# Attention with three PSUM banks for scores, three for the products behind the exponentials, and exponentials of 512 columns

## The reference, cut to what matters

```python
def _rmsnorm_global(x, scale):
    rms = jnp.sqrt(jnp.mean(x * x))
    return x / (rms + EPS) * scale
q, k, v = jnp.split(x @ Wqkv, 3, axis=-1)      # each reshaped to b, s, 16 heads, 16
q = _rmsnorm_global(q, scale_q)
k = _rmsnorm_global(k, scale_k)
attn = jnp.einsum('bqhd,bkhd->bhqk', q, k)
attn = jax.nn.softmax(attn, axis=-1)
z = jnp.einsum('bhqk,bkhd->bqhd', attn, v)
return z.reshape(b, s, d) @ Wo
```

## Time and profile before

| | |
|---|---|
| median of 3 runs | 1784.2 us (1782.71 to 1784.86) |
| profiled execution, its time | 1782.6 us |
| its span, first to last instruction | 1780.8 us |
| TensorE matmul busy | 1558.5 us, 88% of the span |
| VectorE busy | 859.6 us, 48% |
| ScalarE busy | 766.6 us, 43% |
| GpSimd busy | 488.2 us, 27% |
| mean granted TensorE clock | 0.931 |
| second attention | from 1010 to 1291 us of the span |

### The profile page before, as it was taken

The page is one execution under the profiler, slowest core; times in us unless marked ns, Lnnn a source line. Parts: engine busy times, 40 slices in busy tenths (PEclk is TensorE's granted clock), DMA queues, the critical chain, the costliest instruction groups (busy, mean ns, idle before and its releaser), DMA issues.

```text
span 1780.8 us, 19192 instructions
## 1 busy us (share of the span) xinstructions
PE 1558.5 (88%) x7128; PEld 881.8 (50%) x7128; DVE 859.6 (48%) x885; ACT 766.6 (43%) x1176; POOL 488.2 (27%) x139
## 2 busy tenths in 40 slices
PE   5887896698989987799887588888799999999998
PEld 3775333687979784554343222222254444444443
DVE  4994757698989886544430676666210000000000
ACT  1232565798989872113232146556622122122221
POOL 0996200398879790401022200000000000000000
PEclk7799898899999998589999689999989999999999
DMA  3000003122231115110100651111000000000000
GB/s 143 16 10 1 24 25 146 45 84 95 105 108 62 48 37 213 29 18 18 35 35 36 116 222 53 41 53 36 1 0 1 0 12 0 0 12 0 12 0 12
DMA packets 32078, 84.84 MB, mean 48 GB/s; under 512 B 5091, under 2 KB 21569, under 8 KB 29569
## 3 DMA queue, kind: packets, MB, share of 16 engines
q1 hardware_dynamic: 30081, 82.21, 13.5%
q10 hardware_dynamic: 1920, 1.57, 0.6%
HBM read 66.79 MB, written 16.91 MB: 47 GB/s over the span
## 4 chain that ended last, share of the span: by engine, by line
PE 55%; POOL 16%; DVE 9%; issue 8%; ACT 4%; DVEq 4%; DMA 1%; ACTq 1%; SPq 0%; POOLq 0%
POOL arena L2049 15%; PE ps L1223 13%; PE ps L1238 12%; PE ps L1095 3%; DVE mxs L1922 3%; PE ps L1007 3%; PE ps L1135 2%; PE ps L1075 2%; PE ps L1049 2%; DVE arena L1623 2%; PE ps L751 2%; DVEq L1622 2%; POOL arena L2029 2%; ACT arena L1548 1%; PE ps L964 1%
## 5 line engine op out<-in xcount | busy, mean ns | idle before, releaser
L2049 POOL TENSOR_TENSOR arena<-arena 128x2048 f32<-128x2048 f32 x64 | 289.9, 4559 | 166.6 <-DVE arena L1722 166.6
L1722 DVE TENSOR_TENSOR_SCAN arena<-arena,ps 128x1024 f32<-128x1024 f32 x128 | 283.9, 2270 | 45.7 <-issue 23.2
L1223 PE MATMUL ps<-arena 128*128 128x512 f32 x512 | 242.3, 599 | 0.0
L1238 PE MATMUL ps<-arena 128*128 128x512 f32 x512 | 239.3, 592 | 0.0
L1590 ACT ACTIVATE arena<-ps,arena 128x512 f32<-128x512 f32 x128 | 87.9, 687 | 349.4 <-PE ps L1223 349.3
L1922 DVE TENSOR_REDUCE mxs<-ps 128x1 f32<-128x512 f32 x256 | 162.0, 684 | 71.5 <-PE ps L1075 70.0
L1424 ACT ACTIVATE arena<-arena,mam 128x511 f32<-128x511 f32 x256 | 165.2, 708 | 33.3 <-DVE arena L1722 33.3
L1548 ACT ACTIVATE arena<-ps,rho 128x1024 f32<-128x1024 f32 x128 | 140.4, 1110 | 90.3 <-PE ps L1135 90.1
L2009 DVE SCALAR_TENSOR_TENSOR arena<-ps,b2s,arena 128x512 f32<-128x512 f32 x8 | 5.6, 747 | 334.4 <-PE ps L1238 334.4
L1223 PEld LDWEIGHTS ps<-arena 128*128 128x128 f32 x512 | 98.0, 192 | 121.9 <-issue 121.9
L1238 PEld LDWEIGHTS ps<-arena 128*128 128x128 f32 x512 | 97.3, 190 | 122.5 <-issue 122.5
(11 more groups left out here) (291 smaller groups left out, 1910.4 us busy)
## 6 DMA issues: line engine op xcount, KB each, us to landing
arena<-bc_scratch SPq DMA_DIRECT2D x32, 512.0 KB, 3.6
batch_scratch<-arena SPq DMA_DIRECT2D x2, 3072.0 KB, 9.1
arena<-batch_scratch SPq DMA_DIRECT2D x6, 1024.0 KB, 7.6
arena<-q_scratch SPq DMA_DIRECT2D x96, 64.0 KB, 2.1
arena<-in_cond SPq DMA_DIRECT2D x1, 5019.5 KB, 23.9
arena<-k_scratch SPq DMA_DIRECT2D x72, 64.0 KB, 2.1
mam<-in_ids SPq DMA_DIRECT2D x4, 768.0 KB, 7.3
q_scratch<-arena SPq DMA_DIRECT2D x4, 768.0 KB, 3.3
```

What stands on the lines that cost most here:

```text
L1223: last = pe.matmul(ps[:, 2 + f % 4, :], w1[:, c, f * P:(f + 1) * P], y4[:, b if isinstance(b, int) else bass.ds(b, 1), c, :], start=(c == ...
L1238: last = pe.matmul(ps[:, 6 * turn + o, :], w2[:, f - 2, o * P:(o + 1) * P], hid[:, (f - 2) % 4, :], start=(f == 2), stop=(f == FM + 1))
L1722: dve.tensor_tensor_scan(half, view(decay[:, (2 * k + h) % 3], [[1, 2 * S]]), view(ps[:, FEED + 2 * h, :], [[1, 2 * S]]), 0.0, ALU.mult, A ...
L2049: pool.tensor_tensor(state[:, k % SLOTS], state[:, k % SLOTS], view(c_rows[:, j % 2, k % G, :], [[0, M], [1, S]]), ALU.mult).then_inc(s_hc, 1)
```

## The change

The six banks are shared out anew: scores go to banks 0, 1 and 2 in turn, the products behind the exponentials to banks 3, 4 and 5 in turn. TensorE now alternates one product and one score, each product counts in `s_t_mm` by itself and waits for the exponential three before it, and each score for the maximum three before it. Exponentials are taken one bank at a time, 512 columns, and `s_pt` counts 16 in a group instead of 8. Sixteen isn't a multiple of three, so the turn is shifted by hg; at hg = 0 it starts anew, and the first product and the first score of that group wait for the one just before them. The counts that others wait for (SP's head loads, the matmul after the stage, `values`, `max_rows`) are adapted.

```diff
@@ SP: heads of the next batch
-                        sp.wait_ge(s_t_mm, g * 8 + 8)
+                        sp.wait_ge(s_t_mm, g * 16 + 16)
@@ TensorE: scores
-                pe.wait_ge(s_max, (b * HG + hg) * 16 + s + 1)
-                pe.matmul(ps[:, s % 2, :], qstack[0:STACK, hg, i, qc * P:(qc + 1) * P], kstack[0:STACK, hg, i, :],
+                if not isinstance(b, int) or b or hg or s > 2:
+                    pe.wait_ge(s_max, (b * HG + hg) * 16 + s + (1 if hg + s == 0 else -1))
+                pe.matmul(ps[:, (hg + s) % 3, :], qstack[0:STACK, hg, i, qc * P:(qc + 1) * P], kstack[0:STACK, hg, i, :],
                           start=True, stop=True).then_inc(s_s_mm, 1)
@@ TensorE: max_rows, values
-                pe.wait_ge(s_max, g * 16 + 18)
+                pe.wait_ge(s_max, g * 16 + 17)
...
-                pe.wait_ge(s_pt, g * 8 + 2 * kc + 4)
+                pe.wait_ge(s_pt, g * 16 + 4 * kc + 7)
@@ TensorE: attend
-                        pe.wait_ge(s_pt, g * 8 + j + 1)
                         for i in (2 * pair, 2 * pair + 1):
-                            last = pe.matmul(ps[:, 2 + 2 * pair + i % 2, :], kstack[0:STACK + 1, hg, i, kc * P:(kc + 1) * P],
-                                             qstack[0:STACK + 1, hg, i, :], start=True, stop=True)
-                        last.then_inc(s_t_mm, 1)
-                        if not (final and hg >= 2):
-                            scores(*ahead, 2 * j)
-                            scores(*ahead, 2 * j + 1)
+                            n = 4 * kc + i
+                            pe.wait_ge(s_pt, g * 16 + n + (3 if hg + n == 0 else 1))
+                            pe.matmul(ps[:, 3 + (hg + n) % 3, :], kstack[0:STACK + 1, hg, i, kc * P:(kc + 1) * P],
+                                      qstack[0:STACK + 1, hg, i, :], start=True, stop=True).then_inc(s_t_mm, 1)
+                            if not (final and hg >= 2):
+                                scores(*ahead, n)
@@ ScalarE: weigh (act.sem_inc(s_pt, 2) at the start becomes 3)
-                        n = g * 8 + j
-                        act.wait_ge(s_t_mm, n + 1)
-                        act.wait_ge(s_pv, g * TILES + j // 2)
-                        act.activation(pt[:, j % 4], ps[:, 2 + 2 * (j % 2):4 + 2 * (j % 2), :], ACT.Exp,
-                                       scale=rho[:, 0:1]).then_inc(s_pt, 1)
+                        for i in range(2):
+                            n = 2 * j + i
+                            act.wait_ge(s_t_mm, g * 16 + n + 1)
+                            act.wait_ge(s_pv, g * TILES + j // 2)
+                            act.activation(pt[:, j % 4, i], ps[:, 3 + (hg + n) % 3, :], ACT.Exp,
+                                           scale=rho[:, 0:1]).then_inc(s_pt, 1)
@@ VectorE: maximum (dve.sem_inc(s_max, 2) at the start becomes 1)
-                dve.tensor_reduce(mxs[:, hg % 2, qc, i:i + 1], ps[:, s % 2, :], AX, ALU.max).then_inc(s_max, 1)
+                dve.tensor_reduce(mxs[:, hg % 2, qc, i:i + 1], ps[:, (turn + s) % 3, :], AX, ALU.max).then_inc(s_max, 1)
```

More of the change, by code:

```diff
@@ L1186, in _ @@
             pe.wait_ge(s_ew, 16)
-            pe.wait_ge(s_pt, B * HG * 8 + 2)
+            pe.wait_ge(s_pt, B * HG * 16 + 3)
             for o in range(C):
@@ L1526, in _ @@
             act.activation(rho[:, :], rho[:, :], ACT.Exp, scale=0.5).then_inc(s_rho_root, 1)
-            act.sem_inc(s_pt, 2)
+            act.sem_inc(s_pt, 3)
             act.wait_ge(s_kp, B + 1)
@@ L1916, in _, with maximum @@
             dve.reciprocal(rho[:, 0:1], rho[:, 0:1]).then_inc(s_rho, 1)
-            dve.sem_inc(s_max, 2)
-            def maximum(hg, n, s):
+            dve.sem_inc(s_max, 1)
+            def maximum(hg, turn, n, s):
                 i, qc = s % HG, s // HG
                 dve.wait_ge(s_s_mm, n + s + 1)
-                dve.tensor_reduce(mxs[:, hg % 2, qc, i:i + 1], ps[:, s % 2, :], AX, ALU.max).then_inc(s_max, 1)
+                dve.tensor_reduce(mxs[:, hg % 2, qc, i:i + 1], ps[:, (turn + s) % 3, :], AX, ALU.max).then_inc(s_max, 1)
             def normalise(g, hg):
@@ L1942, in follow @@
                         if not (final and hg >= 2):
-                            maximum(hg, (g + 2) * 16, s)
+                            maximum(hg, (hg + 2) % HG, (g + 2) * 16, s)
                         if s in (7, 9) and hg == 1 and not first:
@@ L1950, in _ @@
                 for s in range(16):
-                    maximum(hg, hg * 16, s)
+                    maximum(hg, hg, hg * 16, s)
             follow(0, True, False)
```

## The result

The changed kernel takes 1763.03 us (median of 4 runs, 1762.3 to 1764.99) against 1784.53 for the kernel before in the same comparison: ratio 0.988, 95% interval 0.9864 to 0.9895. That is 21.5 us less; the forecast was 24.8 less, 1759.4 with a range of 1753 to 1770.

A forecast was written before the change was run, and what follows sets the result against it. TensorE was taken as the bound, stalling on maxima and exponentials. Gains 18.0 + 1.9 + 3.0 + 2.0 - 0.4 = 24.5, say 24.8, off the 1784.2 us median gave 1759.4, range 1753 to 1770.

The forecast's parts named there:

- ten plain groups: Second attention's groups with scores and no projection: 15.00 us each to 13.20, gain 18.0, 0.3 more for four slightly longer.
- three with hg 1: Three second-attention groups with the output projection: last values at 19.65 us after the first product, before 20.29; gain 1.9.
- first scores: The 32 scores ahead of the second attention's first product: three banks save 1.31 and 1.69 us, gain 3.0.
- group 0: Second attention's first group, clock at 0.50 for 3.4 us again: 15.18 us down to 13.1 to 13.2, gain 2.0.
- last two groups: Groups 14 and 15, without scores: last values move from 11.66 to 11.84 us after the first product, loss 0.4 together.
- s: Spacing between starts of successive 512-column exponentials on ScalarE: taken as 0.577 us, bounds 0.502 and 0.687.
- The rival without overlap: Short exponentials on ScalarE don't overlap, spacing 0.687 us: 9.6 us more, 1769.0; chance 0.16 for no or partial overlap.
- V(0): The four products with the values of key chunk 0: start 3.12 us after a plain group's first product, before 3.72.
- the three excesses: Plain-group delays of 1.12, 0.78 and 0.35 us before the first three sets of value products, put down to two score banks.
- The clock otherwise: TensorE's clock falls at pauses ahead of projections in hg 1 groups: none gives 1757.9, all three 1762.4; chance 0.06.
- Slower, or no gain left: Two rivals on short exponentials' spacing: at 0.90 us 1794, chance 0.03; at 0.82 us 1782 to 1786, chance 0.03.
- the formula: Plain group's length from the exponentials' spacing: past 0.70 us it is 8.20 plus 8 spacings, reaching 15.0 at 0.85.

The follow-up runs named there:

- the split: Kernel before with exponentials of 512 columns and products waiting one by one, its order and banks kept: 1783.4 us, ratio 0.9983.
- the version with two score banks: Changed kernel with scores in banks 0 and 1 only, products still in three banks in turn: 1779.4 us, ratio 0.9963.
- the last version: Changed kernel with the next group's first product and score ahead of the last values, and its exponential ahead of the copy of the sums: 1760.3 us, ratio 0.9843.
- the early product: Changed kernel with the next group's first product and score issued ahead of a group's last values: 1768.0 us, ratio 0.9896.

## Why the prediction was right, step by step

The ladder of a plain group, from the runs: 15.00 before; 14.94 with the split; 14.29 with the alternating order; 14.29 with three product banks; 13.39 with three score banks. The forecast priced the order and the third score bank together and was right that the two score banks held TensorE up; it didn't say that the order alone gives two fifths.

| term | forecast | measured, first trace of each |
|---|---|---|
| ten plain groups | 18.0 + 0.3 | 16.3 (150.28 to 133.96) |
| three with hg 1 | 1.9 | 0.8, and 1.7 for the fall in group 13 that is gone |
| first scores | 3.0 | 3.2 (22.69 to 19.51) |
| group 0 | 2.0 | 0.6 (15.18 to 14.61) |
| last two groups | -0.4 | -0.2 |
| sum | 24.8 | 22.4 |

The terms are right in kind, and most of the gains came out smaller. That the sum comes so near is in part luck: 1.7 of the 22.4 is a fall of the clock that this trace of the kernel before had and the changed one not. What follows the stage then took 4.9 us more, and the medians still ended 21.5 apart.

**Exponentials.** 0.69 and s = 0.577 were forecast, 0.688 and 0.576 came. The rival without overlap (1769) falls.

**Plain groups, mis-sized by 0.19 each.** V(0) was forecast at 3.12 and came at 3.10; V(1), V(2), V(3) at 6.29, 9.46, 12.20 and came at 6.37, 9.66, 12.40. From V(1) on TensorE's own work sets the pace, and I counted a value product as starting 0.217 after the score ahead of it. It starts about 0.31 after it: the last scores before V(1) and V(2) are at 1123.69 and 1126.98, V(1) and V(2) at 1124.00 and 1127.29. The kernel before shows the same, with V(0) at 1134.86:

```profile
1134.54 0.39 PE L1075 MATMUL ps<-arena 96*128 96x512 bf16 x1 [0.15 <-DVE mxs L1922]
```

The number was in its trace and left out of the sum. It also means that of each of the three excesses that the prediction puts down to the two score banks, 0.1 was this gap. The last piece, V(2) to V(3), was forecast at 2.74 and is 2.74.

**Groups with hg 1, mis-sized by 0.38 each.** The second transposes came 3.58 after T0 as forecast, but each step behind them is a little later: an exponential behind transposes starts 0.50 after its product, not 0.42, V(0) starts at 5.04 (4.95 forecast), the projection at 9.15 (8.99), V(1) at 11.93 (11.68), V(2) at 17.28 (16.91). Each step is a latency of 0.1 us or so; I took the shortest seen for all of them.

**Group 0, the step that failed.** "With the clock at 0.50 for 3.4 us again": it lasted 6.3. At 0.50 the matmuls of 512 columns start 0.43 apart (1027.43 to 1032.12, twelve of them), TensorE alone is the bound, and order and third bank help nothing there; V(0) came at 5.26 (4.4 to 4.5 forecast). Counted from the first maximum, the clock rose at 25.8 us, near the 26.1 of before. But the first scores were 3.2 us shorter, so the first product stood 3.2 us earlier against that rise, and group 0 had 2.9 us more at 0.50. By the prediction's own "each us of it at 0.50 costs half a us" that is 1.45, and 1.4 is what the term missed. So in this pair of traces nearly half of what the first scores gave was lost again in group 0, a coupling that the sum doesn't have. It isn't the whole story: the five traces with three score banks have the rise 25.6 to 25.8 after the first maximum, of the five with two score banks two have it at 26.1 and three at 29.1. Against the trace of the kernel before with 29.1 (16.10 to V(3)) the gain is 1.5. What sets the rise stays open.

**The clock otherwise.** I gave three pauses a chance of a fall at 1.5 us each. Both traces of the kernel before have one fall in the stage (1.7). Neither trace of the changed kernel has one, nor have the split alone, the alternating order, the version with two score banks and the last version; those with exponentials of 256 and with the early product have four. So it isn't shown that the change keeps the clock up. What follows the stage, the same instructions in all, took 491.2 and 494.3 us in the kernel before and 489.4 to 496.1 in the others, and by and large the longer it took, the more of it was granted 0.50 (14.9 us for 489.4, 30.5 for 496.1). In the first pair of traces that takes 4.9 us of the 22.4 gained, and the earlier start gives 2.9 back. The 496.1 stands in both traces of the changed kernel, but in the split alone too, whose stage is only 2 us shorter than before, while the version with two score banks has 491.1. So it goes with none of the edits.

**Slower, or no gain left.** The slower rival needed exponentials 0.85 apart; the run with exponentials of 256 shows the mechanism real. At its 0.713 the formula gives 8.20 + 8 x 0.713 = 13.90 for a plain group and the run has 14.52; a tile made in two parts also ends later (0.36 + 0.49 after its start instead of 0.69), which the formula doesn't hold. These 0.16 at four places of the group make 14.54. Exponentials 0.85 apart were never run, so the slower time itself is not shown.

## What to carry to other kernels

Where two rings share a fixed number of banks, count for each how long its slot is held against how often one is wanted, and test each bank by itself: here the fourth product bank was worth nothing and the third score bank 0.90 us a group. Put the producer's two streams in alternation before buying banks; here it gave 0.65 of 1.6 and no term got worse by it. If an early part of a stage runs at half clock, what is saved there can in part be lost again as half-clock work in the next, where the rise of the clock doesn't come earlier too. An engine idle a fifth of the time can still be on the path at the start and end of each group: moving one exponential ahead of a copy was worth one whole spacing.

## What the runs showed of the hardware

TensorE's clock falls at places that move by tens of microseconds between executions of one kernel (1252 and 1186 in the kernel before), and the time of parts that nobody changed moves with it (491.2 and 494.3 us behind the stage of one kernel, 489.4 to 496.1 over all ten traces). So differences of 0.2% between such kernels are read from lengths of like stretches at full clock, which repeat to about 0.01 us, rather than from whole times.
